# Output product of an attention in two halves of its contraction, the first half placed among the last values and sums

## The reference, cut to what matters

```
q, k, v  = split(h @ w_qkv.T + b_qkv)            # 16 heads of 16 channels
score    = causal(q k^T with a decay and a line bias per head)
P        = exp(score - max);  sum = P.sum(-1)
att[h]   = (P[h] @ v[h]) / sum[h]                # 16 heads side by side: 256 channels
x        = x + att @ w_out.T + b_out
```

## Time and profile before

| what | value |
|---|---|
| median of 3 runs | 2452.81 us |
| lowest, highest | 2452.31, 2461.68 us |
| profiled execution's own time | 2462.85 us |
| its span | 2461.1 us |
| TensorE matmul busy | 2076.2 us, 84% |
| VectorE busy | 1315.3 us, 53% |
| ScalarE busy | 1015.5 us, 41% |
| GpSimd busy | 860.7 us, 35% |
| mean granted TensorE clock | 0.887 |

### The profile page before, as it was taken

How to read it: one execution, slowest core, us unless ns; L and a number is a source line. 1 busy time by engine, 2 the same in 40 slices (tenths; PEclk the granted TensorE clock), 3 DMA queues, 4 the chain that set the end, 5 groups by cost and what they waited for, 6 DMA issues and landing times. The chain is left out here.

```text
span 2461.1 us, 33853 instructions
## 1 busy us (share of the span) xinstructions
PE 2076.2 (84%) x11838; PEld 1320.1 (54%) x11838; DVE 1315.3 (53%) x3698; ACT 1015.5 (41%) x2503; POOL 860.7 (35%) x594
## 2 busy tenths in 40 slices
PE   5518889889889889889889879889999498888897
PEld 5305555555555565565565455457778345454545
DVE  2356757757757656756766663422111156565635
ACT  2005446636536545545645645522222132323231
POOL 0172626336346246246347340131000251515121
PEclk9658698889889888888888889999999699899999
DMA  7100020021021030030030030043455320202000
GB/s 259 46 0 20 1 72 27 1 89 27 1 91 25 1 100 16 1 106 9 3 104 9 9 104 36 26 161 116 148 172 191 110 71 5 83 5 83 6 25 18
DMA packets 67453, 146.09 MB, mean 59 GB/s; under 512 B 16356, under 2 KB 42074, under 8 KB 62946
## 3 DMA queue, kind: packets, MB, share of 16 engines
q1 hardware_dynamic: 51434, 93.79, 11.2%
q0 software_dynamic: 15872, 50.35, 7.0%
HBM read 114.64 MB, written 29.46 MB: 59 GB/s over the span
## 5 line engine op out<-in xcount | busy, mean ns | idle before, releaser
L1257 ACT ACTIVATE att_buf<-att_buf,nmin 128x384 f32<-128x384 f32 (+3 forms) x512 | 288.4, 563 | 410.3 <-DVE nmin L1622 410.1
L1041 PE MATMUL bank<-kk,qT 32*128 32x512 f32 (+2 forms) x1024 | 297.2, 622 | 37.2 <-DVE nmin L1622 36.6
L778 POOL TENSOR_TENSOR big<-ex_at,kx 128x2048 f32<-128x2048 f32 x64 | 235.9, 3714 | 171.5 <-DVE xt_na L1367 133.4
L1074 PE MATMUL bank<-ident,att_buf 128*128 128x128 f32 x1280 | 229.4, 308 | 59.3 <-ACT att_buf L1265 58.7
L1611 DVE TENSOR_TENSOR att_buf<-bank,wdiag 128x128 f32<-128x128 f32 x384 | 93.1, 284 | 245.0 <-PE bank L1046 243.7
L1265 ACT COPY att_buf<-bank 128x384 f32<-128x384 f32 (+3 forms) x512 | 210.8, 412 | 29.1 <-PE bank L1088 26.9
L1088 PE MATMUL bank<-att_buf,vp 128*32 128x128 f32 x2560 | 220.4, 310 | 0.0
L725 POOL TENSOR_TENSOR big<-kx 128x1280 f32<-128x1280 f32 x64 | 162.6, 2575 | 161.8 <-ACT kx L1155 143.3
L1074 PEld LDWEIGHTS bank<-ident,att_buf 128*128 128x128 f32 x1280 | 160.2, 158 | 79.2 <-ACT att_buf L1257 78.2
L790 POOL DMA_INDIRECT buf_d<-nB,sidx x64 | 62.7, 980 | 355.1 <-DVE sidx L1486 338.0
L1088 PEld LDWEIGHTS bank<-att_buf,vp 128*32 128x32 f32 x2560 | 137.0, 121 | 55.1 <-issue 45.3
(11 more groups left out here) (352 smaller groups left out, 4039.0 us busy)
## 6 DMA issues: line engine op xcount, KB each, us to landing
big<-in_eW SPq DMA_DIRECT2D x16, 1024.0 KB, 7.6
kk<-in_eW SPq DMA_DIRECT2D x16, 1024.0 KB, 7.6
buf_d<-zero SPq DMA_DIRECT2D x8, 640.0 KB, 7.6
xt_na<-in_xT SPq DMA_DIRECT2D x8, 512.0 KB, 3.4
nA<-in_xN SPq DMA_DIRECT2D x8, 512.0 KB, 3.6
x_d<-x SPq DMA_DIRECT2D x8, 512.0 KB, 3.3
x<-x_d SPq DMA_DIRECT2D x8, 512.0 KB, 4.0
out<-qf SPq DMA_DIRECT2D x8, 512.0 KB, 2.9
```

The source lines that it names most:

```text
L778: pool.tensor_tensor(pv[:, c * P:(c + 1) * P, :].rearrange("p (h d) o -> p o h d", d=DH), spread(ex[:, t, :, 8 * c:8 * c + 8], 3, DH), spr ...
L1041: pe.matmul(bank[u % 2][:, 0:n], qT[r:r + 32, g, i * P:(i + 1) * P], kk[r:r + 32, g, T * i * P:T * i * P + n], start=True, stop=False)
L1074: mm = pe.transpose(bank[3 + u % 2][:, j * P:(j + 1) * P], pr[:, u % NPR, j * P:(j + 1) * P], ident[:])
L1257: act.activation(pr[:, u % NPR, 0:n], pr[:, u % NPR, 0:n], ACT.Exp, scale=-1.0, bias=nmin[:, u % 4:u % 4 + 1], accum_out=rsum[:, i, h:h + ...
```

## The change

The output product is issued in two parts by its contraction. `out_half(m, *ts)` issues contraction half m for the token tiles ts. Half 0, which needs only `att_ok` 1, is spread over the tail: tile 0 behind the transposes of `turn_sums(1)`, tiles 1 and 2 behind `values(62)`, tile 3 behind `broadcast_sums(1)`. Half 1, the other 8 of the 16 matmuls, follows the wait for `att_ok` 2, and `out_mm` comes behind tiles 1 and 3 as before. A wait for `max_ok` N stands ahead of the first part, since banks 0 and 1 must have been read. The start flag is set on the first matmul of a bank only. Instructions outside TensorE's program are the same.

```diff
 if b2 is not None:
+    def out_half(m, *ts):
+        pe.wait_ge(s("att_ok"), m + 1)
+        for t in ts:
+            mm = pe.matmul(bank[t // 2][:, (t % 2) * D:(t % 2 + 1) * D], aT2[:, m, t * P:(t + 1) * P],
+                           wout[:, m, :], start=(m == 0 and t % 2 == 0), stop=(m == K2 - 1 and t % 2 == 1))
+        return mm
+
     turn_sums(1)
+    pe.wait_ge(s("max_ok"), N)
+    out_half(0, 0)
     values(N - 2)
+    out_half(0, 1, 2)
     broadcast_sums(1)
-
-    pe.wait_ge(s("att_ok"), 2)
+    out_half(0, 3)
     for c in range(2):
-        for t in (2 * c, 2 * c + 1):
-            for m in range(K2):
-                mm = pe.matmul(bank[c][:, (t % 2) * D:(t % 2 + 1) * D], aT2[:, m, t * P:(t + 1) * P],
-                               wout[:, m, :], start=(m == 0), stop=(m == K2 - 1))
-        mm.then_inc(s("out_mm"), 1)
+        out_half(1, 2 * c, 2 * c + 1).then_inc(s("out_mm"), 1)
```

## The result

The changed kernel takes 2427.07 us (median of 5 runs, 2425.26 to 2435.57), the kernel before 2452.81 us (5 runs, 2448.41 to 2461.68). The ratio is 0.990, interval 0.9878 to 0.9921: 25.7 us faster.

A forecast was written before the change was run, and what follows sets the result against it. TensorE's matmuls, filling 84% of the span, were taken to bound the kernel. Three tails at 0.55 and five at 1.1 save 7.1 us, from the 2452.81 median to 2446 us; own range 2441 to 2449, with rivals 2437 to 2461.

The forecast's parts named there:

- Where the time was looked for: Tail of each of 8 attention iterations: TensorE idles 0.85 us ahead of L1144 while half its matmuls could run earlier.
- The gap of 0.2 and 0.1: Ahead of the broadcast: each inserted waiting group costs 0.2 us for its load and 0.1 for the next one's gap.
- The count of instructions ahead of the broadcast: Tile 0 as one matmul, tiles 1 and 2 as two, 0.22 us each; with gaps the broadcast is 0.9 us late.
- Tile 3: Behind the broadcast: one matmul with its load, 0.4 us, hidden in TensorE's 0.85 us idle before the divide's end.
- full-clock tail: Tails 1, 2 and 7, output product at 2.4 GHz: second addition 0.5 us earlier, 0.6 in tail 7; summed at 0.55.
- Tails at 1.2 GHz: Five of eight tails, output product at clock 0.50: second addition 1.1 us earlier, 1.7 without gaps.
- The step that failed: Sum over tails: 3 at 0.55 and 5 at 1.1 give 7.1 us, range 4 to 12, nothing for the remaining body.
- Rival A: Loop bodies: the clock takes back the saving inside the loop, only tails 0 and 7 gain, 1.7 us; 2451 us, chance 0.26.
- Rival B: Tails: filled gaps end the slow output product and shorten slow stretches behind the barrier, 15.3 us; 2437 us, chance 0.16.
- Rival C: Loop bodies: cutting the batch of 16 idles TensorE, one more slow stretch in each of six; 2466 us, chance 0.12.

The follow-up runs named there:

- e1_fill: Changed kernel's half 0 in the gaps, plus the whole 16-matmul product behind the divide, so half 0 is computed twice; 2467.54 us, 0.9895 of the kernel before.
- e2_late: Changed kernel with all of half 0 behind the broadcast, beside the divide, and nothing ahead of it; 2488.22 us, 0.9985 of the kernel before.
- e7_second: Changed kernel with only tiles 1 and 2 ahead of the broadcast, tiles 3 and 0 behind it; 2466.42 us, 0.9873 of the kernel before.
- e12_endfill: Changed kernel plus three unused products (six instructions) behind its last product, beside VectorE's additions; 2442.83 us, 0.9772 of the kernel before.
- e5: Changed kernel with tiles 0 and 1 ahead of and between the last two turns, 2 and 3 behind the broadcast; 1.0036 of the kernel before.
- e6: Changed kernel with tile 0 left in place and tiles 1, 2, 3 behind the broadcast; 1.0027 of the kernel before.
- group 2: Second set of follow-up runs, sharing one chip: both kernels unaltered and two other placements of half 0; the changed kernel there took 2487.74 us, 0.9998.
- c3_after: The changed kernel, unaltered, as a second control on another chip; 2471.02 us, 0.9891 of the kernel before.
- c4_after: The changed kernel, unaltered, as control on the chip of e7_second and e12_endfill; 2465.86 us, 0.9867 of the kernel before.

## Why the prediction was wrong

**Where the time was looked for: right.** The tail was the place, the chain of the earlier trace rows was read correctly, VectorE's additions follow as foreseen, and from the second addition's end to the next body's first matmul it is still 2.6 us (511.10 to 513.74), so GpSimd did not become the end.

**The gap of 0.2 and 0.1: right for tiles 1 and 2, luck for tile 0.** Values were forecast 0.96 us behind the first transpose and are at 0.96 to 0.97. But tile 0 is two instructions, 0.44 us and not 0.22, streamed by 504.48, and the values start at 504.57: the gap is 0.09 and not 0.3. Two errors of about 0.2 cancelled. Around tiles 1 and 2 the gaps are 0.09 and 0.18 us (values streamed by 505.04, next start 505.13; four instructions streamed by 506.01, broadcast 506.19), together 0.27 for the 0.3 taken. The weight load of tile 0 came without a gap (503.93), that of the group behind it shows 0.33 us, most of it beside matmuls in flight. The rule taken from the Trainium skill, "TensorE: Matmul & The Clock Gate", section "Architectural detail: the array is 16× 32×32, not 1× 128×128", fits the first load and not the second.

**The count of instructions ahead of the broadcast: wrong.** L1144 is x16 for 4 tiles by 2 halves, so a tile's half is two instructions. The prediction put eight behind the divide, which is right, but took tile 0 as one, tiles 1 and 2 as two and tile 3 as one: four are missing, three of them ahead of the broadcast. Tile 0's is the one that its smaller gap hid. Tiles 1 and 2 cost 4 x 0.22 = 0.88 where 0.43 stood, and the broadcast is late by 1.33 us and not 0.9. Tile 3's two are hidden as foreseen: the second half starts at 508.16, 0.05 us behind the divide's end. From the divide's end to the second addition it is 2.31 us, forecast 2.4. So a full-clock tail goes from 6.99 to 6.82, a gain of 0.17 and not 0.55. By its own mechanism the forecast should have been smaller.

**Tails at 1.2 GHz: wrong in kind.** Forecast was a product that stays at 0.50 and a gain of 1.1 us. None stays there: 8.56 to 6.82 is 1.74. Added over the eight tails, 2.0 + 2 x 0.17 + 4 x 1.74 + 0.4 = 9.7 us, for 7.1 forecast.

**The step that failed** is the one that made this the end of the sum. The forecast took the rest of the body as unchanged: in its sum that term is nothing, and what the clock does there is left to rivals A and B. By the medians the gain is 25.7 us; the tails explain 9.7, so 16 came from where the forecast had none. Rival B was right about its mechanism, that three tiles in the gaps keep the clock at the output product (e1_fill against e2_late on one chip; e7_second for the place: tiles 1 and 2 are enough); it had 0.16. But B too priced only the tail and what lies right behind the barrier, 15.3 us. That last piece came in part. It gave tails 1 and 2 a slow stretch behind the barrier as short as that of the earlier trace rows in place of the earlier trace rows. Behind tail 1 it is still 6.5 us long; behind tails 2 to 5 it is 3.3, which those behind tails 3 to 5 had before as well. These stretches of the changed kernel are behind tail 1 and behind tail 3:

```profile
513.70:516.80 3.10, 3.06 (x11) 3.07 (x12) 2.86 (x14) 1.22 (x2) 1.08 (x4) 0.50 0.61 200
517.00:520.30 3.30, 3.30 (x15) 3.30 (x15) 2.31 (x6) 0.00 (x0) 1.54 (x2) 0.50 0.50 182
...
868.60:871.80 3.20, 3.20 (x11) 3.20 (x12) 3.05 (x14) 1.15 (x2) 1.03 (x4) 0.50 0.65 206
871.90:875.00 3.10, 3.10 (x23) 2.93 (x22) 2.01 (x6) 0.22 (x2) 1.02 (x2) 1.00 0.50 181
```

What nobody priced is the remaining body, where 17.1 of the 20.5 us at 0.50 lay that went in all (44.4 to 23.9), and four bodies got 6.8 us shorter each, 1.7 of it in the tail.

**Rival A** rested on the earlier trace rows, equal lengths with the product at either clock. They were a sign that a body's length hangs on the clock along the whole body; read as "what is won is given back", they pointed the wrong way. The second body after is 180.8 with a full-clock tail, just as A has it; the four behind it are 174.1.

**Rival C** expected harm from a batch of 16 cut into pieces, and cited the Trainium skill, "Perfetto Trace Analysis", section "Matmul Optimizations". That the engine scales with its use speaks for the change once the idle time between the pieces is looked at instead of the batch: the pieces fill it. The runs agree with the rule in that form: e1_fill and e12_endfill do more work in less time.

**What stays open.** That the gain goes with the clock and not with the tail's length is shown by the experiments; why the stretches far from the tail (912 to 934 us, 1022 to 1042) turn to 1.00 is not, beyond the lengths that recur. Which places of a tail must be filled is shown only in part: e7_second shows that tiles 1 and 2 are enough; that anything is needed ahead of the broadcast rests on e2_late, since e5 and e6 ran on the chip where the change gains nothing. The -9.3 us ahead of the first loop body and the -5.0 in layer 1 lie nearly all in instructions that are the same, and no run separated them. On one of the four chips on which the changed kernel was measured it was worth nothing (0.9998); three of its tails were slow there, and the later values explain only part of it. The first chip wasn't measured again.

## What to carry to other kernels

When TensorE's clock moves between its two levels and the matmuls bound the kernel, price an edit also by what it does to TensorE's idle time, and look beyond the edited place: up to half of each microsecond at 1.2 GHz is at stake along the loop, here 5.1 us of a body beside 1.7 in its tail. Work that can stand in a wait belongs there even where it delays the chain a little, and a few matmuls that nobody reads, placed in an unavoidable wait, are worth a trial (0.992 alone, 0.9772 with the change). Count instructions in the trace, not calls in the source, before multiplying.

## What the runs showed of the hardware that was not expected

**ScalarE stops in the loop tails.** A loop tail of c_before, the unaltered kernel before, on the chip of group 2:

```profile
1230.68 0.37 ACT L1265 COPY att_buf<-bank 128x256 f32<-128x256 f32 x1
...
1235.51 0.37 ACT L1265 COPY att_buf<-bank 128x256 f32<-128x256 f32 x1 [4.46 <-remote]
...
1236.92 0.58 ACT L1274 COPY gb<-bank 8x512 f32<-8x512 f32 x1 [1.03 <-remote]
...
1237.55 2.07 PE L1103 MATMUL bank<-gb,sel 8*128 8x512 f32 x2 [0.59 <-ACT gb L1274]
...
1240.47 6.57 PE L1144 MATMUL bank<-wout,cat 128*128 128x256 f32 x16 [0.85 <-DVE cat L1598]
```

Between two copies that follow each other directly in the earlier trace rows ScalarE idles for 4.46 us, released by what the profile calls "remote", and everything behind it is at 0.50. In c3_after it is 2.92 us:

```profile
1052.66 0.37 ACT L1271 COPY att_buf<-bank 128x256 f32<-128x256 f32 x1 [2.92 <-remote]
...
1054.09 2.08 PE L1140 MATMUL bank<-wout,cat 128*128 128x256 f32 x4
...
1058.19 1.99 PE L1140 MATMUL bank<-wout,cat 128*128 128x256 f32 x8 [0.22 <-DVE cat L1604]
```

There tiles 1 and 2 run at 0.50 (2.08 us for 1.13), the second half at full clock. The stop is in the loop tails of every trace from the five later chips, and in their tail 7, in no tail of the first two traces, and never in tail 0. What causes it is not known; it is the likeliest part of the 40 us by which the kernel before is slower on those chips, which is not shown.

**Unused matmuls pay.** e12_endfill does 48 matmul instructions more than c4_after on the same chip and is 23 us faster (2442.83 for 2465.86).
